# Output projection in two passes for the first and last chunk only, in whole tiles for the two in between; second passes and two last-projection tiles moved

## The chip, the cores and the metric

The kernel runs on all 8 NeuronCores of one Trainium2 chip. Each core takes one of the 8 sequences (2048 tokens of width 1024), so the cores do the same work on other data and do not talk to each other. The time is device microseconds of the slowest core, the median of several executions. TensorE (PE in the rows) multiplies, VectorE (DVE) and ScalarE (ACT) read its results out of the eight PSUM banks, GpSimd (POOL) works on SBUF alone, and SyncE (SP) issues the DMAs.

## The reference, cut to what matters

```python
def ffn(x):                      # rank-256 feed-forward, hidden width 4096
    P = x @ U1
    H = gelu(P @ V1 + b1)
    Q = H @ U2
    return Q @ V2 + b2
x = x + 0.5 * ffn(layernorm(x))
y = layernorm(x)                 # attention: 16 heads of 64, causal
q, k, v = y @ Q_w + Q_b, y @ K_w + K_b, y @ V_w + V_b
attn = softmax(mask(q @ k.T / 8)) @ v
x = x + attn @ O_w + O_b         # the output projection: 1024 x 1024
x = x + 0.5 * ffn(layernorm(x))
```

## The kernel before, in words

Everything is held transposed, features on partitions and tokens along the row. The 2048 tokens are four **chunks** of 512; a 1024-wide row is eight blocks of 128 features, so `x[:, c, m, :]` is chunk c, block m. A matmul has at most 512 columns, which fill one PSUM bank.

The kernel has three stages: a first feed-forward (chunk by chunk), attention (two heads at a time, eight **head pairs** p = 0 to 7), and a second feed-forward. Each engine has its own queue, filled by the Python program in a fixed order; an engine runs its queue strictly in that order, and a wait stops everything behind it on that engine.

**Attention** goes in 40 **rounds** to a head pair. Round k issues the scores of two key tiles (`qk_step`, line 1036), ScalarE's exponential of them (line 1049), and, three rounds late (`LAG`), the product with V (`av_step`, line 1074). Scores use banks 0 to 3, so the scores of round i wait for the exponential of round i-2. The products use banks 4 and 5. At the end of one head of one chunk ScalarE takes the logarithm and the exponential of the sums (lines 1090 and 1095) and VectorE multiplies them in (line 1099, `multiply`). In the last pair the chunks come in order: chunk 0 has rounds 0 to 3, chunk 1 rounds 4 to 11, chunk 2 rounds 12 to 23, chunk 3 rounds 24 to 39. ScalarE has more to do in a round than TensorE, so other TensorE work is pulled into the rounds from a generator (`window`, in the last pair `window7`), by shares that `spread` works out in units of one 512-column matmul. That work uses banks 6 and 7: `main_bank` takes them in turn, `side_bank` names the other one.

**The output projection** needs all eight pairs: 32 tiles (c, m) of eight matmuls, one for each pair. Before the change every tile has two passes: `o_most` does the seven pairs that are there early and VectorE adds bank and bias to x (line 1242); `o_last` does the matmul of the last pair when its chunk is ready (line 1250), and VectorE adds that too (line 1252). `o_last` starts for chunks 0, 1 and 2 at rounds 9, 17 and 29 (`O_GATE`), for chunks 1 and 2 also not before the normalisation of chunk 0 has come to its stage 3; between two `o_last` an `o_most` is issued as long as there are any. The last two of the 32 `o_most` are kept for the end, after round 39. The eight `o_last` of chunk 3 follow them: five at once, three in the first steps of the feed-forward.

In between, `window7` also prepares the second feed-forward for chunk 0: `ln3_cast` (VectorE's copy to bf16, line 179, and GpSimd's square, line 187) for every two blocks, two sums on TensorE (`ln_sum`, line 195), and the projection with U1 (line 227).

**The second feed-forward** takes 32 **steps** to a chunk. Step g has two V1 matmuls (lines 254 and 256) into bank g mod 3, ScalarE's gelu (line 261), and two U2 matmuls for step g-2 (line 271) into banks 3 and 4. `put(c, s, ...)` hangs further work on step s of chunk c, behind its V1 matmuls and ahead of its U2 matmuls. The last projection of chunk c-1 (`out_tile`: two V2 matmuls at lines 289 and 291, VectorE's sum at line 296, and the store of the result) hangs on steps 4 to 11 of chunk c. `f2_stat` at step 18 and `f2_break` at step 21 normalise the next chunk: ScalarE leaves its gelu table for logarithm and exponential, TensorE does 16 U1 matmuls, VectorE scales them out of banks 6 and 7 (line 237).

Of the kernel before, what the change touches and what calls it, by code (L numbers as in the profile page):

```python
# [17 lines left out]
NP = 8  # L18
# [67 lines left out]
def build_nc(debug=()):  # L86
# [1033 lines left out]
    def window(p):  # L1120
# [8 lines left out]
        if p == NP - 2:  # L1129
            mains += [(lambda: o_most(*o_left.popleft())) for _ in range(3)]  # L1130
        after = {}
# [95 lines left out]

    def o_most(c, m):

        b = main_bank()  # L1230
        PE.need(t_wo[m], bank_free[b])
        t = None
        for k in range(NP - 1):
            PE.need([t_at[k, c, h] for h in range(2)])
            f = lambda e, k=k: e.matmul(ps[:, b, :], wo[:, m, k, :], attn[:, c, k, :], start=(k == 0), stop=(k == NP - 2))  # L1235
            if k < NP - 2:
                PE.run(f)
                yield 1
            else:
                t = PE.do(f)  # L1240
        DVE.need(t, t_cols)
        bank_free[b] = DVE.do(lambda e: e.scalar_tensor_tensor(  # L1242
            x[:, c, m, :], ps[:, b, :], cols[:, C_OB + m:C_OB + m + 1], x[:, c, m, :], OP.add, OP.add))
        yield 1

    def o_last(c, m, b=None):

        b = main_bank() if b is None else b
        PE.need(t_wo[m], bank_free[b], [t_at[NP - 1, c, h] for h in range(2)])
# [23 lines left out]

    o_left = collections.deque((c, m) for c in range(NCH) for m in WO)

    O_GATE = (9, 17, 29)

    def window7():


        last = collections.deque((c, n) for c in range(NCH - 1) for n in range(NM))
        stage, since, k1 = 0, 0, {}
        while o_left or last or stage < 6:
            moved = False
            if last and rounds[0] >= O_GATE[last[0][0]] and (last[0][0] == 0 or stage >= 3):
                c, n = last.popleft()
                assert (c, WO[n]) not in o_left
                yield from o_last(c, WO[n])
                if n % 2 and c < 2:
                    ln3_cast(c, WO[n] // 2)  # L1290
                if (c, n) == (0, NM - 1):
                    stage, since = 1, 0
                moved = True
            if stage == 1 and since >= 3:
                b1 = main_bank()
# [18 lines left out]
            elif stage in (4, 5) and since >= 2:  # L1314
# [6 lines left out]
                stage, since, moved = stage + 1, 1, True  # L1321
            if o_left and (len(o_left) > 2 or rounds[0] >= 40):
                yield from o_most(*o_left.popleft())
                since += 1
                moved = True
            if not moved:
# [49 lines left out]
    for i in range(len(steps) + LAG + 3):  # L1376
        if i < len(steps):
            p, c, h, r, n, it = steps[i]
            k = i - 40 * p
            if k == 0:  # L1380
# [163 lines left out]
```

How the kernel before makes its waits and increments, by code:

```python
    def need(self, *tokens):  # L41
        for t in tokens:
            if t is None:
                continue
            if isinstance(t, list):
                self.need(*t)
                continue
            sem, val = t
            if self.passed.get(id(sem), 0) >= val:
                continue
            self.passed[id(sem)] = val
            self.items.append(lambda e, sem=sem, val=val: e.wait_ge(sem, val))
# [1 line left out]
    def do(self, fn):  # L54
        self.n += 1
        self.items.append(lambda e, fn=fn: fn(e).then_inc(self.sem, 1))
        return (self.sem, self.n)
# [21 lines left out]
    def load(self, q, out, src):  # L80
        self.n += 16
        q.items.append(lambda e, out=out, src=src: e.dma_start(out, src).then_inc(self.sem, 16))
        return (self.sem, self.n)
```

## Time and profile before

| | |
|---|---|
| times of 3 runs, us | 876.78, 876.81, 903.51; median 876.81 |
| the profiled execution | 876.68 us, its slowest core's span 875.1 us (core 7) |
| spans of the 8 cores | 871.3 to 875.1 us |
| busy in that span | PE 821.2 us (94%), DVE 466.4 us (53%), ACT 636.8 us (73%), POOL 167.0 us (19%) |
| first scores of the last head pair | 613.10 us from the start |
| first U2 matmuls of the second feed-forward | 722.23 us from the start |

The profiled execution's own time is 1.6 us above its span, and 0.1 us from the median. A matmul's busy time (379 ns for 512 columns) overlaps the next one's: back to back they start 216 ns apart. So a hole between two of them is best counted from start to start, less 216 ns for each matmul in between; the idle time that a row prints in brackets is 0.16 us shorter.

### The profile page before, as it was taken

The numbers are of one execution on the slowest core, as the hardware profiler recorded it, in microseconds if no ns is written. First come the engines' busy times: TensorE is split into PE (matmuls) and PEld (weight loads), VectorE is DVE, ScalarE is ACT, GpSimd is POOL, SyncE is SP. The second block draws the span as 40 slices with busy tenths as digits, with TensorE's granted clock in tenths as the row PEclk, the third lists the DMA queues.
The fourth block names the chain that finished last, engine by engine and source line by source line (L and its number), as shares of the span: only waits on it lengthen the run. The fifth ranks groups of instructions, "written<-read, shape, count | busy, mean of one in ns | idle before, by whom it ended". The sixth has DMA issues, their size and how long they took to land.

```text
span 875.1 us, 13105 instructions; the slowest of 8 cores (871.3 to 875.1 us)
## 1 busy us (share of the span) xinstructions
PE 821.2 (94%) x4122; PEld 397.4 (45%) x4122; DVE 466.4 (53%) x735; ACT 636.8 (73%) x803; POOL 167.0 (19%) x192
## 2 busy tenths in 40 slices
PE   4899999999899999999999999999989969999997
PEld 1344444444445455464554545544434424444442
DVE  2466665656565744746447474374553470445352
ACT  2667675768566898999999898989646526766764
POOL 0220400003231212313123131221231220031100
PEclk9899999999999999999999999999999999999999
DMA  8899301000041002200012000227000010122122
GB/s 266 265 324 322 54 2 49 1 2 1 1 119 40 1 1 55 78 25 1 1 61 73 25 1 1 75 73 239 26 1 1 1 41 8 46 64 88 22 97 96
DMA packets 17929, 57.83 MB, mean 66 GB/s; under 512 B 2116, under 2 KB 3524, under 8 KB 17352
## 3 DMA queue, kind: packets, MB, share of 16 engines
q1 hardware_dynamic: 17864, 57.00, 21.6%
q8 instruction: 36, 0.59, 0.3%
q14 instruction: 29, 0.24, 0.1%
HBM read 43.35 MB, written 13.64 MB: 65 GB/s over the span
## 4 chain that ended last, share of the span: by engine, by line
PE 85%; DVE 6%; ACT 4%; issue 3%; DMA 1%; DVEq 0%; SPq 0%; POOL 0%; ACTq 0%; POOLq 0%
PE ps L1036 13%; PE ps L271 13%; PE ps L1074 12%; PE ps L673 12%; PE ps L254 6%; PE ps L256 6%; PE ps L822 6%; PE ps L1235 6%; PE ps L195 4%; PE ps L227 2%; ACT pt L1049 2%; PE ps L730 1%; PE ps L289 1%; PE ps L291 1%; DMA x<-x 1%
## 5 line engine op out<-in xcount | busy, mean ns | idle before, releaser
L1049 ACT ACTIVATE pt<-ps,small 128x1024 bf16<-128x1024 f32 x320 | 321.8, 1026 | 97.6 <-PE ps L1036 91.3
L261 ACT ACTIVATE hb<-ps,cols 128x512 bf16<-128x512 f32 x256 | 171.3, 686 | 80.2 <-PE ps L256 79.3
L1036 PE MATMUL ps<-QZ,KM 128*128 128x512 bf16 (+1 forms) x640 | 177.1, 358 | 2.0 <-ACT pt L1049 1.8
L1074 PE MATMUL ps<-pt,V 128*128 128x512 bf16 (+3 forms) x640 | 170.3, 348 | 0.9 <-POOL V L884 0.9
L1058 POOL TENSOR_TENSOR pt<-pt,cb 128x256 bf16<-128x256 bf16 x128 | 87.3, 694 | 335.6 <-ACT pt L1049 335.6
L673 PE MATMUL ps<-yb,wqk 128*128 128x512 bf16 x512 | 140.3, 382 | 4.2 <-DVE small L734 1.5
L1074 PEld LDWEIGHTS ps<-pt,V 128*128 128x128 bf16 x640 | 62.5, 98 | 66.6 <-issue 2.1
L1036 PEld LDWEIGHTS ps<-QZ,KM 128*128 128x128 bf16 x640 | 61.1, 98 | 61.8 <-issue 13.7
L271 PE MATMUL ps<-hb,u2b 128*128 128x512 bf16 x256 | 76.5, 384 | 3.7 <-ACT hb L261 2.1
L271 PE MATMUL ps<-hb,u2c 128*128 128x512 bf16 x256 | 75.3, 379 | 1.8 <-ACT hb L261 1.4
L822 PE MATMUL ps<-wvb,yb 128*128 128x256 bf16 x512 | 73.5, 272 | 1.9 <-DVE small L734 1.2
L673 PEld LDWEIGHTS ps<-yb,wqk 128*128 128x128 bf16 x512 | 48.5, 98 | 53.0 <-issue 8.4
L296 DVE SCALAR_TENSOR_TENSOR x<-ps,small,x 128x512 f32<-128x512 f32 x64 | 47.2, 749 | 35.9 <-PE ps L291 35.8
L696 DVE TENSOR_SCALAR QZ<-ps,cols 64x512 bf16<-64x512 f32 x64 | 47.9, 748 | 33.5 <-PE ps L673 32.1
L734 DVE TENSOR_REDUCE small<-ps 128x1 f32<-128x512 f32 x64 | 44.1, 689 | 34.4 <-PE ps L730 33.9
L1235 PE MATMUL ps<-attn,wo 128*128 128x512 bf16 x224 | 57.1, 379 | 4.7 <-DVE x L1242 4.7
L822 PEld LDWEIGHTS ps<-wvb,yb 128*128 128x128 bf16 x512 | 49.0, 99 | 25.8 <-issue 3.9
L1099 DVE TENSOR_TENSOR attn<-ps,LR 64x512 bf16<-64x512 f32 x64 | 44.0, 688 | 30.9 <-ACT LR L1095 28.3
L254 PE MATMUL ps<-pb,v1b 128*128 128x512 bf16 x128 | 50.0, 390 | 3.3 <-DVE small L465 3.3
L256 PE MATMUL ps<-pb,v1b 128*128 128x512 bf16 x128 | 49.9, 390 | 0.0
L256 PE MATMUL ps<-pb,v1c 128*128 128x512 bf16 x128 | 48.5, 379 | 0.0
L254 PE MATMUL ps<-pb,v1c 128*128 128x512 bf16 x128 | 48.5, 379 | 0.0
(134 smaller groups left out, 876.5 us busy)
## 6 DMA issues: line engine op xcount, KB each, us to landing
x<-x SPq DMA_DIRECT2D x16, 512.0 KB, 13.2
out<-x SPq DMA_DIRECT2D x32, 256.0 KB, 2.4
stg<-u SPq DMA_DIRECT2D x10, 512.0 KB, 10.9
stg<-v SPq DMA_DIRECT2D x10, 512.0 KB, 10.8
wos<-wo SPq DMA_DIRECT2D x8, 512.0 KB, 4.2
wst<-wq SPq DMA_DIRECT2D x7, 512.0 KB, 4.0
wst<-wk SPq DMA_DIRECT2D x7, 512.0 KB, 4.3
wst<-wv SPq DMA_DIRECT2D x6, 512.0 KB, 10.2
```

What stands on the lines that cost most here:

```text
L254: PE.run(lambda e: e.matmul(ps[:, b, :], F["v1"][:, fc // 4, 0, 128 * (fc % 4):128 * (fc % 4 + 1)], F["pb"][:, c % 2, 0, :], start=True, s ...
L256: t = PE.do(lambda e: e.matmul(ps[:, b, :], F["v1"][:, fc // 4, 1, 128 * (fc % 4):128 * (fc % 4 + 1)], F["pb"][:, c % 2, 1, :], start=Fals ...
L261: F["t_gelu"][g] = ACT.do(lambda e: e.activation(F["hb"][:, g % 4, :], ps[:, b, :], AF.Gelu_apprx_tanh, bias=cols[:, C_B1 + fc:C_B1 + fc + ...
L271: f = lambda e, m=m: e.matmul(ps[:, 3 + m, :], F["u2"][:, fc, 128 * m:128 * (m + 1)], F["hb"][:, g % 4, :], start=(fc == 0), stop=(fc == N ...
L673: f = lambda e, k=k: e.matmul(ps[:, b, :], wqk[:, which, k, :], yb[:, ch, k, :], start=(k == 0), stop=(k == NM - 1))
L696: toks.append(DVE.do(lambda e, r=r, h=h: e.tensor_scalar(QZ[s][r, h, csl], ps[r, b, :], cols[r, C_QB + p:C_QB + p + 1], None, OP.add)))
L822: f = lambda e, k=k, kt=kt, o=o: e.matmul(ps[:, b, o:o + 256], yb[:, kt // 4, k, 128 * (kt % 4):128 * (kt % 4 + 1)], wvb[:, k, :], start=( ...
L1036: f = lambda e, j=j, kt=kt: e.matmul(ps[:, 2 * sl + j, lo:TC], KM[s][:, 128 * kt:128 * (kt + 1)], QZ[s][:, h, TC * c + lo:TC * (c + 1)], s ...
L1049: t_e[i] = ACT.do(lambda e: e.activation(pt[:, i % 4, :, lo:TC], ps[:, 2 * sl:2 * sl + 2, lo:TC], AF.Exp, bias=bias, scale=0.125))
L1058: L["pt", i] = POOL.do(lambda e, v=v: e.tensor_tensor(v, v, mask, OP.mult))
L1074: f = lambda e, kt=kt, lo=lo, j=j: e.matmul(ps[:, b, lo:TC], V[gr % 2][:, kt, pr, 64 * h:64 * h + 128], pt[:, i % 4, j, lo:TC], start=(kt ...
L1235: f = lambda e, k=k: e.matmul(ps[:, b, :], wo[:, m, k, :], attn[:, c, k, :], start=(k == 0), stop=(k == NP - 2))
```

## The change

- `o_most` becomes `o_tile(c, m, np)`, which does seven pairs or all eight. Chunks 1 and 2 are now done in whole tiles of eight matmuls with one addition on VectorE, from rounds 17 and 29 on. Chunks 0 and 3 keep their two passes (3 of the 16 first passes lie in pair 6 as before, 11 in the last pair ahead of the rest, and two are again kept for the end).
- The eight second passes of chunk 0 are no longer between tiles: they go inside a first pass, after its third and sixth matmul, into `side_bank`; when no first pass is left they go one after the other.
- The casts of chunk 1 for the normalisation are kept back until chunk 0 has reached stage 3. The waits in units between the stages of chunk 0 are two instead of three for the first.
- In the last three rounds two units are pulled instead of seven.
- The eight second passes of chunk 3 all hang on steps of the feed-forward's chunk 0: 3, 4, 5, 6, 22, 22, 23, 23.
- `out_tile` of blocks 6 and 7 moves from steps 10 and 11 to steps 22 and 23, both into bank 5, for the chunks 0 and 1 (which are put out during chunks 1 and 2).

```diff
@@ window
         if p == NP - 2:
-            mains += [(lambda: o_most(*o_left.popleft())) for _ in range(3)]
+            mains += [(lambda: o_tile(*o_most.popleft())) for _ in range(3)]
@@ the tile and the second pass
-    def o_most(c, m):
+    def o_tile(c, m, np=NP - 1):
         b = main_bank()
         PE.need(t_wo[m], bank_free[b])
         t = None
-        for k in range(NP - 1):
+        for k in range(np):
             PE.need([t_at[k, c, h] for h in range(2)])
-            f = lambda e, k=k: e.matmul(ps[:, b, :], wo[:, m, k, :], attn[:, c, k, :], start=(k == 0), stop=(k == NP - 2))
-            if k < NP - 2:
+            f = lambda e, k=k: e.matmul(ps[:, b, :], wo[:, m, k, :], attn[:, c, k, :], start=(k == 0), stop=(k == np - 1))
+            if k < np - 1:
                 PE.run(f)
                 yield 1
             else:
                 t = PE.do(f)
...
     def o_last(c, m, b=None):
-        b = main_bank() if b is None else b
+        b = side_bank() if b is None else b
@@ window7
-    o_left = collections.deque((c, m) for c in range(NCH) for m in WO)
+    o_most = collections.deque((c, m) for c in (0, NCH - 1) for m in WO)
+    O_END = 2
...
-        last = collections.deque((c, n) for c in range(NCH - 1) for n in range(NM))
+        full = collections.deque((c, m) for c in range(1, NCH - 1) for m in WO)
+        last = collections.deque(WO)
...
+        def last_one():
+            m = last.popleft()
+            yield from o_last(0, m)
+            if m % 2:
+                ln3_cast(0, m // 2)
+            if not last:
+                stage, since = 1, 0
...
-            if o_left and (len(o_left) > 2 or rounds[0] >= 40):
-                yield from o_most(*o_left.popleft())
+            while held and stage >= 3:
+                ln3_cast(1, held.popleft())
+            tile = None
+            if full and rounds[0] >= O_GATE[full[0][0]]:
+                c, m = full.popleft()
+                tile = o_tile(c, m, NP)
+            elif o_most and (len(o_most) > O_END or rounds[0] >= 40):
+                c, m = o_most.popleft()
+                tile = o_tile(c, m)
+            if tile is not None:
+                for u, _ in enumerate(tile):
+                    yield 1
+                    if u in (2, 5) and last and rounds[0] >= O_GATE[0] and (0, last[0]) not in o_most:
+                        yield from last_one()
+                if c == 1 and m % 2:
+                    held.append(m // 2)
                 since += 1
+                moved = True
+            elif last and rounds[0] >= O_GATE[0] and (0, last[0]) not in o_most:
+                main_bank()
+                yield from last_one()
                 moved = True
@@ the rounds after the last
-            pull(acc + 7)
+            pull(acc + 2)
@@ ahead of and in the second feed-forward
-    for n, b in enumerate((6, 7, 4, 3, 5)):
-        go(o_last(3, WO[n], b))
...
-    for n, b in ((5, 5), (6, 6), (7, 7)):
-        put(0, n - 4, lambda n=n, b=b: go(o_last(3, WO[n], b)))
+    for n, (g, b) in enumerate(((3, 5), (4, 6), (5, 7), (6, 5), (22, 5), (22, 6), (23, 7), (23, 5))):
+        put(0, g, lambda n=n, b=b: go(o_last(3, WO[n], b)))
     for c in range(NCH):
         if c >= 1:
             for m in range(8):
-                put(c, 4 + m, out_tile, c - 1, m, (7, 5, 6)[m % 3])
+                put(c, 4 + m if m < 6 else 16 + m if c + 1 < NCH else 4 + m, out_tile, c - 1, m,
+                    (7, 5, 6)[m % 3] if m < 6 or c + 1 == NCH else 5)
```

The line numbers of the changed kernel are a little higher: its tiles are at line 1236 with VectorE's sum at line 1243, its second passes at line 1254 with the sum at line 1256, its `mean_in` at line 1479.

**VectorE, rounds 9 to 12 of the last pair** (the second passes of chunk 0). `TENSOR_TENSOR x<-ps,x` is the sum of a second pass, `SCALAR_TENSOR_TENSOR x<-ps,cols,x` that of a first pass, `CAST xb3a<-x` the copy of two blocks for the normalisation, `attn<-ps,LR` is `multiply`. Before:

```order
L1242 SCALAR_TENSOR_TENSOR x<-ps,cols,x 128x512
L1252 TENSOR_TENSOR x<-ps,x 128x512
L179 CAST xb3a<-x 128x1024
L1242 SCALAR_TENSOR_TENSOR x<-ps,cols,x 128x512
L1252 TENSOR_TENSOR x<-ps,x 128x512
L1099 TENSOR_TENSOR attn<-ps,LR_81 64x512
```

Now:

```order
L1243 SCALAR_TENSOR_TENSOR x<-ps,cols,x 128x512
L1256 TENSOR_TENSOR x<-ps,x 128x512 x2
L179 CAST xb3a<-x 128x1024
L1243 SCALAR_TENSOR_TENSOR x<-ps,cols,x 128x512
L1256 TENSOR_TENSOR x<-ps,x 128x512 x2
L179 CAST xb3a<-x 128x1024
L1243 SCALAR_TENSOR_TENSOR x<-ps,cols,x 128x512
L1256 TENSOR_TENSOR x<-ps,x 128x512 x2
L1099 TENSOR_TENSOR attn<-ps,LR_81 64x512
```

A first pass's sum now stands behind a second pass's sum and a cast; before, it stood ahead of the second pass.

**TensorE, rounds 10 to 12**, where the second passes of chunk 0 lie. `L1036` are the scores of a round, `L1074` the product with V of three rounds earlier, `L1235` (now `L1236`) first-pass matmuls, `L1250` (now `L1254`) second passes. Before:

```order
L1235 MATMUL ps<-attn,wo 128x512 x2
L1250 MATMUL ps<-attn,wo 128x512
L1235 MATMUL ps<-attn,wo 128x512 x4
L1036 MATMUL ps<-QZ_71,KM_73 128x256 x2
L1074 MATMUL ps<-pt,V_70 128x512 x2
L1235 MATMUL ps<-attn,wo 128x512 x3
L1250 MATMUL ps<-attn,wo 128x512
L1235 MATMUL ps<-attn,wo 128x512 x3
```

Now:

```order
L1236 MATMUL ps<-attn,wo 128x512
L1254 MATMUL ps<-attn,wo 128x512
L1236 MATMUL ps<-attn,wo 128x512 x4
L1254 MATMUL ps<-attn,wo 128x512
L1036 MATMUL ps<-QZ_71,KM_73 128x256 x2
L1074 MATMUL ps<-pt,V_70 128x512 x2
L1236 MATMUL ps<-attn,wo 128x512 x3
L1254 MATMUL ps<-attn,wo 128x512
L1236 MATMUL ps<-attn,wo 128x512
L1254 MATMUL ps<-attn,wo 128x512 x2
```

Before, every second pass stood between two first passes. Now of the four first-pass matmuls in one piece the first ends a tile and the other three begin the next, in the other bank; the second pass behind them goes to the bank of the tile that has just ended. Two second passes of round 12 follow behind that round's scores and product, and no first pass is left.

**TensorE, rounds 13 to 17.** Before, rounds 13 to 16 had six to eight matmuls each beside the attention's. Now:

```order
L1074 MATMUL ps<-pt,V_70 128x256
L1074 MATMUL ps<-pt,V_70 128x128
L1036 MATMUL ps<-QZ_71,KM_73 128x512 x2
L1074 MATMUL ps<-pt,V_70 128x512 x2
L1036 MATMUL ps<-QZ_71,KM_73 128x512 x2
L1074 MATMUL ps<-pt,V_70 128x512 x2
L1036 MATMUL ps<-QZ_71,KM_73 128x256 x2
L1074 MATMUL ps<-pt,V_70 128x512 x2
L1236 MATMUL ps<-attn,wo 128x512 x16
L195 MATMUL ps<-xb3a,cb 128x512 x8
L1236 MATMUL ps<-attn,wo 128x512 x10
```

Rounds 13 to 16 have nothing beside the attention's matmuls, and round 17 has 34 others in one piece.

**TensorE, from the last round to the feed-forward's first U2 matmuls** (`L254` and `L256` are its V1 matmuls, `L271` its U2 matmuls). Before:

```order
L1235 MATMUL ps<-attn,wo 128x512 x7
L1074 MATMUL ps<-pt,V_70 128x512
L1074 MATMUL ps<-pt,V_70 128x384
L1235 MATMUL ps<-attn,wo 128x512 x7
L1074 MATMUL ps<-pt,V_70 128x256
L1074 MATMUL ps<-pt,V_70 128x128
L1250 MATMUL ps<-attn,wo 128x512 x5
L254 MATMUL ps<-pb_88,v1c 128x512
```

Now:

```order
L1236 MATMUL ps<-attn,wo 128x512 x2
L1074 MATMUL ps<-pt,V_70 128x512
L1074 MATMUL ps<-pt,V_70 128x384
L1236 MATMUL ps<-attn,wo 128x512 x2
L1074 MATMUL ps<-pt,V_70 128x256
L1074 MATMUL ps<-pt,V_70 128x128
L1236 MATMUL ps<-attn,wo 128x512 x10
L254 MATMUL ps<-pb_88,v1c 128x512
```

Ten matmuls of first passes now stand behind the last product, where five second passes stood; the first second pass of chunk 3 comes after the eight V1 matmuls of steps 0 to 3.

## Rows read from the trace of the kernel before

**Rows 1.** The page: chain that ended last, by engine.

```profile
PE 85%; DVE 6%; ACT 4%; issue 3%; DMA 1%; DVEq 0%; SPq 0%; POOL 0%; ACTq 0%; POOLq 0%
```

**Rows 2.** Timeline of TensorE: start us, duration us, engine, line, operation, count.

```profile
613.10 0.59 PE L1036 MATMUL ps<-QZ,KM 128*128 128x512 bf16 x2
...
619.64 1.89 PE L1235 MATMUL ps<-attn,wo 128*128 128x512 bf16 x8
```

**Rows 3.** Timeline of all engines, around one second pass of chunk 0.

```profile
651.53 0.69 DVE L179 CAST xb3a<-x 128x1024 bf16<-128x1024 f32 x1
...
652.92 0.59 PE L1235 MATMUL ps<-attn,wo 128*128 128x512 bf16 x2
653.35 0.38 PE L1250 MATMUL ps<-attn,wo 128*128 128x512 bf16 x1
653.62 0.75 DVE L1242 SCALAR_TENSOR_TENSOR x<-ps,cols,x 128x512 f32<-128x512 f32 x1 [0.67 <-PE ps L1235]
...
654.52 0.81 PE L1235 MATMUL ps<-attn,wo 128*128 128x512 bf16 x3 [0.79 <-DVE x L1242]
```

**Rows 4.** Waits between 610 and 720 us: who waited, for whom, total us, times, longest.

```profile
PE ps L1235 <- DVE x L1242: 4.7, 6, 0.8
...
PE ps L1250 <- DVE x L1252: 3.0, 6, 1.6
```

**Rows 5.** Timeline, second passes of chunks 1 and 2.

```profile
705.73 1.19 PE L1250 MATMUL ps<-attn,wo 128*128 128x512 bf16 x2 [1.61 <-DVE x L1252]
```

**Rows 6.** Windows: stretch, length, each engine's busy us (x), granted clock, DMA.

```profile
706.00:707.00 1.00, 0.99 (x4) 0.44 (x4) 0.76 (x2) 0.00 (x0) 1.00 (x1) 0.50 0.00 0
...
760.00:780.00 20.00, 20.00 (x94) 9.11 (x93) 10.04 (x13) 10.98 (x17) 7.84 (x4) 1.00 0.35 119
```

**Rows 7.** Timeline, from the last product of attention to the feed-forward.

```profile
714.28 0.33 PE L1074 MATMUL ps<-pt,V 128*128 128x256 bf16 x2
...
714.76 0.59 ACT L1090 ACTIVATE LR<-ps 64x512 f32<-64x512 f32 x1 [6.64 <-PE ps L1074]
...
717.01 1.24 PE L1250 MATMUL ps<-attn,wo 128*128 128x512 bf16 x5 [2.40 <-DVE attn L1099]
...
717.38 0.20 ACT L1425 ACTIVATE small<-small 128x1 f32<-128x1 f32 x1
...
720.72 0.38 PE L1250 MATMUL ps<-attn,wo 128*128 128x512 bf16 x1 [1.61 <-DVE x L1252]
...
722.23 1.03 PE L271 MATMUL ps<-hb,u2c 128*128 128x512 bf16 x4
```

**Rows 8.** The page's group of the exponential; timeline of one round's scores and exponential.

```profile
L1049 ACT ACTIVATE pt<-ps,small 128x1024 bf16<-128x1024 f32 x320 | 321.8, 1026 | 97.6 <-PE ps L1036 91.3
...
641.28 0.59 PE L1036 MATMUL ps<-QZ,KM 128*128 128x512 bf16 x2
...
641.97 1.11 ACT L1049 ACTIVATE pt<-ps,small 128x1024 bf16<-128x1024 f32 x1 [2.12 <-PE ps L1036]
```

**Rows 9.** Timeline, end of the feed-forward's chunk 0 (steps 22 to 24).

```profile
745.46 1.29 DVE L237 TENSOR_TENSOR pb<-ps,rstd 128x512 bf16<-128x512 f32 x2 [5.43 <-ACT rstd L219]
745.54 0.38 PE L254 MATMUL ps<-pb,v1c 128*128 128x512 bf16 x1
...
746.22 1.28 ACT L261 ACT_TABLE_LOAD   x1 [0.86 <-PE ps L256]
...
747.51 2.64 ACT L261 ACTIVATE hb<-ps,cols 128x512 bf16<-128x512 f32 x4
...
748.34 0.59 PE L271 MATMUL ps<-hb,u2c 128*128 128x512 bf16 x2 [0.48 <-ACT hb L261]
```

**Rows 10.** Timeline, VectorE's sum of one second pass, the next one, and a V2 tile's sum.

```profile
700.92 0.68 DVE L1252 TENSOR_TENSOR x<-ps,x 128x512 f32<-128x512 f32 x1
...
701.75 0.38 PE L1250 MATMUL ps<-attn,wo 128*128 128x512 bf16 x1 [0.22 <-DVE x L1252]
...
759.71 0.75 DVE L296 SCALAR_TENSOR_TENSOR x<-ps,small,x 128x512 f32<-128x512 f32 x1 [2.21 <-PE ps L291]
```

More of the change, by code:

```diff
@@ L1241, in o_most @@
         DVE.need(t, t_cols)
-        bank_free[b] = DVE.do(lambda e: e.scalar_tensor_tensor(
+        t = DVE.do(lambda e: e.scalar_tensor_tensor(
             x[:, c, m, :], ps[:, b, :], cols[:, C_OB + m:C_OB + m + 1], x[:, c, m, :], OP.add, OP.add))
+        bank_free[b] = t
+        if np == NP:
+            t_x2[c][m] = t
         yield 1
     def o_last(c, m, b=None):
-        b = main_bank() if b is None else b
+        b = side_bank() if b is None else b
         PE.need(t_wo[m], bank_free[b], [t_at[NP - 1, c, h] for h in range(2)])
@@ L1272, in ffn2_weights @@
         F2["t_u1"] = ld_sc[2].load(SP, u1c[:, :, :], s_u1)
-    o_left = collections.deque((c, m) for c in range(NCH) for m in WO)
+    o_most = collections.deque((c, m) for c in (0, NCH - 1) for m in WO)
     O_GATE = (9, 17, 29)
+    O_END = 2
     def window7():
-        last = collections.deque((c, n) for c in range(NCH - 1) for n in range(NM))
-        stage, since, k1 = 0, 0, {}
-        while o_left or last or stage < 6:
-            moved = False
[L1285 to L1294, printed above, removed]
+        full = collections.deque((c, m) for c in range(1, NCH - 1) for m in WO)
+        last = collections.deque(WO)
+        stage, since, k1, held = 0, 0, {}, collections.deque()
+        def last_one():
+            nonlocal stage, since
+            m = last.popleft()
+            assert (0, m) not in o_most
+            yield from o_last(0, m)
[3 more added lines that the diff above has]
+                stage, since = 1, 0
+        while o_most or full or last or held or stage < 6:
+            moved = False
+            if stage == 1 and since >= 2:
                 b1 = main_bank()
@@ L1397, in build_nc @@
                 else:
-                    share = spread(p, 0, 40, 7 * len(o_left) - 14 + 24 + 32)
+                    share = spread(p, 0, 40, 7 * (len(o_most) - O_END) + 8 * 16 + 8 + 32)
             rounds[0] = k if p == NP - 1 else 0
```

## The prediction

> **What bounds the kernel now.** The chain of waits comes first: 85% of the span goes through TensorE [rows 1], and the feed-forwards run it without a hole, 20.00 us of 20.00 at full clock in a stretch of the second [rows 6]. The change touches the last head pair and what follows, so I read TensorE's timeline there. From the pair's first scores at 613.10 [rows 2] to the feed-forward's first U2 matmuls at 722.23 [rows 7] are 109.1 us. A 512-column matmul costs 0.216 us: eight in a row took 1.89, the last one's 0.38 included [rows 2]. The program has the work of 419.5 such matmuls in that stretch (203 first-pass and 32 second-pass matmuls, 16 for sums, 16 U1, 8 V1, and 144.5 for the attention), 90.6 us. So 18.5 us are holes, and the reader should see in the rows that they are of three kinds.
>
> - **A: a tile after a second pass.** VectorE's sum of a first pass starts 0.49 us after the last matmul (652.92 plus 0.22, to 653.62) and the next tile, two banks on and so in the same bank, starts 0.90 us after that; one second pass of 0.22 stands between. The hole is 654.52 - 653.35 - 0.22 = 0.95 [rows 3]. The list of waits has six of this kind for first passes, 4.7 us in brackets [rows 4]; five lie beside chunk 0's second passes, and with one for the U1 matmuls and smaller ones A is 7.4 us.
> - **B: sixteen second passes with hardly a first pass between them**, 700 to 711 us. One matmul of 0.22 needs a sum of 0.68 [rows 10], and two banks don't hide that; the longest single hole is 1.77 us, 1.61 in brackets, where casts stood among the sums [rows 5]. Behind it the granted clock was 0.50, which is 1.2 GHz, and matmuls took twice their time [rows 6]. B is 6.5 us.
> - **C: the end.** The last product ends at 714.28 + 0.16 = 714.44 (call it T). Five second passes wait for the last `multiply` until 717.01, and a sixth for sums until 720.72 [rows 7]. From T to 722.23 are 7.8 us for 16 matmuls, 3.5 us: 4.3 us of holes.
>
> ScalarE waits for TensorE 91.3 us at its exponentials over the whole kernel [rows 8], so in general a hole that closes on TensorE is time won.
>
> **The change part by part.**
>
> *Whole tiles for chunks 1 and 2.* The sixteen second passes, and their sixteen sums, go; the matmuls stay, as eighth of a tile. A bank comes back after 8 matmuls in the other one, 1.7 us, against the 0.49 + 0.90 of A. B goes, and so do the holes of A that don't belong to chunk 0 (one first pass, the U1 matmuls). I leave 0.6 us for small ones (such as a sum held up by a cast of 0.69 [rows 3]). GpSimd's squares and masks are off this path, as the product comes three rounds late.
>
> *The second passes of chunk 0 inside tiles.* They don't get cheaper. Take the order on VectorE: second-pass sum, cast (every second time), first-pass sum. From t = 0, the second of them in round 10: its sum runs 0.48 to 1.16, and 0.15 later the next tile may use its bank (701.60 to 701.75 in [rows 10]), at 1.31; one matmul stood between, so 0.88 us of hole. The cast goes to 1.82, the ended tile's sum to 2.55, so the second pass behind three matmuls starts at 2.70 instead of 1.96: 0.74. Scores, product and three matmuls hide the next. The fourth pass is at 4.21; its sum, its cast and the last first pass's sum end at 6.78, and the fifth starts at 6.93 instead of 4.65: 2.28. The last one waits 0.43 more. Sum 4.3 us, where before the same eight cost 5.1.
>
> *Rounds 13 to 16 without other work.* From the start of round 13's scores to that of round 17's, TensorE has four rounds of scores and four products, two of them short ones at the diagonal: 3.1 us. ScalarE starts an exponential 0.69 us after the scores begin [rows 8], and does three of 1.03 and a logarithm of 0.59 [rows 7] before round 17's scores may start: 0.69 + 3.09 + 0.6 = 4.4. So TensorE loses 1.25 us. It can't be below 0, and is 3 if the other closing steps of chunk 1 and their latencies fall into it too. I take 1.25. The 34 matmuls of round 17 cost nothing: ScalarE waits, and has the time for it afterwards.
>
> *The end.* Behind T now stand ten first-pass matmuls and V1 of steps 0 to 3. ScalarE is through with its table and a small gelu at 717.38 + 0.20, that is T + 3.14 [rows 7]. V1 of step 0 is done by T + 2.6 plus latency, so gelu 0 runs to T + 3.83. V1 of step 3 uses its bank and starts at T + 3.97; ahead of it are 16 matmuls, 3.46: a hole of 0.5. Then 0.43, a second pass of 0.22, and U2 starts at T + 4.6. Of C 4.3 becomes 0.5.
>
> Here the Trainium skill differs from the trace. In the trace a table load is 1.28 us and the next activation follows at once [rows 9]; "ScalarE: Activation LUTs", section "What ACT_TABLE_LOAD costs", has about 2.66 us, because a drain of 1.38 comes on top. By that, an estimate from the page, the hole would be 1.9 instead of 0.5 and the time 1.4 us longer; by this trace there is no such gap.
>
> *The feed-forward.* Seven second passes that were in the stretch are now inside steps: the stretch loses 1.5 us of work and the feed-forward gets it, sum 0. In steps 3 to 6 they have a bank each and VectorE is idle. At the end of a chunk the U2 matmuls of step 22 wait for gelu 22 behind a table load; the hole is 0.48, or 0.64 from start to start [rows 9]. Work of 0.86 us put there is partly free. Chunk 0's four second passes need banks 6 and 7, which VectorE scales until 746.75 [rows 9]; TensorE comes to them at 746.2 and 747.3, so they hardly wait, and U2 starts at 748.63 instead of 748.34: 0.57 won. For chunks 1 and 2 both V2 tiles use bank 5: the first one's sum of 0.75 [rows 10] stands behind the scaling, 746.75 to 747.5, so the second starts at 747.62 instead of 747.26, and U2 at 748.9: 0.3 won each. Together 1.2; between 0 (if the sums come later than this) and 1.9.
>
> **Sum.** The stretch: 412.5 matmuls are 89.1 us, and 4.3 + 1.25 + 0.5 + 0.6 = 6.65 of holes, 95.8 against 109.1: 13.4 less, of which 1.5 has only moved: 11.9. With 1.2, 13.1 us. The profiled execution took 876.7, as the median (876.8), so 863.7.
>
> **The rivals.**
>
> *The holes are larger than worked out, 868 us.* Rounds 10 to 16 have 5.6 us of holes close together. Before, the clock went to 1.2 GHz behind such a stretch (B) and cost 1.7 us; for it speaks that likeness, against it that the holes of A and of C left the clock at full. The Trainium skill, "TensorE: Matmul & The Clock Gate", section "A second HAM failure mode: psum-queue depth-cycling", says that small idle times between groups that cycle through banks can make the clock go up and down; of its two cases here, A and B, the trace has it in B. With the clock 1.7, rounds 13 to 16 at 3 instead of 1.25, and nothing from the feed-forward, 1.2: 868.4. Chance 0.2.
>
> *The second passes of chunk 0 are hidden after all, 859.5.* If VectorE's queue were not in the way, 4.3 us of holes would go. For it: they were put into the other bank, three matmuls and a round's attention apart. Against: the order of casts and sums. Chance 0.09.
>
> *The change doesn't do what it says, 874.* Whole tiles could meet holes as before: if each waits for VectorE 0.6 us, 16 tiles take back 10 of the 13 us. Against: 1.7 us of cover, and 16 sums fewer. Chance 0.04.
>
> *Slower, above 877.* The one mechanism is rounds 12 to 16: TensorE falls to ScalarE's pace, the clock goes to 1.2 GHz and stays there. A matmul then costs twice; from a saving of 13.1 us, it decides when more than 26 us run at 1.2 GHz. In this trace the low clock held about 3.4 us in B, and it rose while matmuls ran densely; the 34 in one piece behind the gap are dense. Chance 0.01.
>
> **How the numbers follow.** The forecast has 0.66. It spans 860.5 to 866.5 by its own bounds: the feed-forward's gain, rounds 13 to 16, and 1.5 us either way on the holes of rounds 10 to 12. The range takes in the larger holes above and most of the hidden case: 859.5 to 869.5. A measurement can tell about 2% from no change, 17.5 us here: faster than 859.3 takes a part of the hidden case and little else, 0.05; slower than 894 needs the last rival, and far more than 26 us of it, under 0.01; the rest, 0.94, is within 2%.
>
> **What the changed profile would show.** No line for second passes between rounds 17 and 39, and no clock of 0.5 near 700; waits of tiles for VectorE's sums only in rounds 10 to 12, one of them 2 us long or more; in rounds 13 to 16 scores waiting for exponentials, about a microsecond in all; U2 4.6 us behind the last product; at the end of chunks 1 and 2 of the feed-forward a V2 matmul that waits a third of a microsecond for a sum. The stretch from the pair's first scores to U2 should be 95.8 us. Wrong would be the step on rounds 10 to 16 above all: it is worked out from an order, and the order of VectorE's and ScalarE's turns moves with every hole.

## The result, and the profile after

| | before | changed |
|---|---|---|
| profiled execution, us | 876.68 | 866.92 |
| span of its slowest core, us | 875.1 | 865.4 |
| spans of the 8 cores, us | 871.3 to 875.1 | 856.2 to 865.4 |
| median, us | 876.8 (3 runs; a fourth, run beside the changed kernel, took 957.03) | 866.2 (4 runs: 865.15, 865.44, 866.92, 956.6) |

The ratio is 0.9869, with a 95% interval of 0.9842 to 0.9895: 1.3% or 11.5 us faster, clear of the noise though less than 2%. It leaves out the runs in a disturbed state of the chip (903.51, 957.03 and 956.6), which both kernels have. The forecast was 863.7 us, ratio 0.985, with 859.5 to 869.5.

Most of the work below goes by two lengths on one core. The **long stretch** is from attention's first scores to the second feed-forward's first U2 matmuls; it holds the last head pair. The **feed-forward** is from there to its last U2 matmuls. Both are read from the starts of the rows, and both repeat from core to core within 0.1 us where the granted clock doesn't fall to 1.2 GHz on the way (the falls come below). Here is the profile of the changed kernel, timeline of TensorE on core 3, which had no such fall:

```profile
203.77 0.59 PE L1036 MATMUL ps<-QZ,KM 128*128 128x512 bf16 x2
...
709.88 0.59 PE L271 MATMUL ps<-hb,u2c 128*128 128x512 bf16 x2
```

709.88 - 203.77 = 506.1 us. Before, on core 5, likewise without a fall (timeline of TensorE):

```profile
202.68 0.59 PE L1036 MATMUL ps<-QZ,KM 128*128 128x512 bf16 x2
...
720.77 0.59 PE L271 MATMUL ps<-hb,u2c 128*128 128x512 bf16 x2
```

518.1 us. So 12.0 us came from the long stretch. The feed-forward got longer by 0.44, from 141.22 to 141.66 us. That is 11.6 us, about the 11.5 of the ratio.

**Where the 12.0 us are.** At the end of attention, timeline of all engines on core 1, the answer to [rows 7]:

```profile
707.44 0.33 PE L1074 MATMUL ps<-pt,V 128*128 128x256 bf16 x2
707.60 2.32 PE L1236 MATMUL ps<-attn,wo 128*128 128x512 bf16 x10
...
709.25 1.28 ACT L1455 ACT_TABLE_LOAD   x1
...
710.54 0.20 ACT L1455 ACTIVATE small<-small 128x1 f32<-128x1 f32 x1
...
710.65 2.41 ACT L261 ACTIVATE hb<-ps,cols 128x512 bf16<-128x512 f32 x4
...
711.47 0.38 PE L254 MATMUL ps<-pb,v1c 128*128 128x512 bf16 x1 [0.25 <-ACT hb L261]
...
712.11 1.03 PE L271 MATMUL ps<-hb,u2c 128*128 128x512 bf16 x4
```

From the last product's end at 707.60 to U2 are 4.5 us instead of 7.8, with one hole of 0.41 (711.47 less 710.84, the start of the last V1 matmul, less 0.22). The ten matmuls cover ScalarE's way to the gelu. The table load ends at 710.53; the small activation and the gelus follow it directly, as in [rows 9].

Between 654 and 707 us TensorE has hardly a hole left. The windows of core 1 answer to [rows 6]:

```profile
646.00:648.00 2.00, 2.00 (x7) 0.61 (x6) 2.00 (x4) 1.12 (x1) 0.49 (x1) 0.55 0.00 0
...
660.00:680.00 20.00, 20.00 (x99) 9.32 (x97) 7.89 (x11) 12.30 (x14) 7.18 (x5) 1.00 0.00 1
690.00:704.00 14.00, 14.00 (x68) 6.43 (x66) 4.49 (x7) 8.60 (x9) 0.14 (x1) 1.00 0.01 2
```

So B is gone, and so are the holes of A from chunk 1 on. But in the first row the clock is 0.55 (1.2 GHz for most of it), at another place than before. On four cores before and two after, it also fell near 224 us, at the start of attention, which made their long stretches 1.6 to 1.8 us longer. The slowest core of each profile had both falls.

What is left stands in rounds 10 to 16, here on core 3 (timeline of TensorE and VectorE; the pattern of before is [rows 3]):

```profile
636.66 0.38 PE L1254 MATMUL ps<-attn,wo 128*128 128x512 bf16 x1
636.87 0.38 PE L1236 MATMUL ps<-attn,wo 128*128 128x512 bf16 x1
637.14 0.69 DVE L1256 TENSOR_TENSOR x<-ps,x 128x512 f32<-128x512 f32 x1 [0.77 <-PE ps L1254]
...
637.94 1.07 DVE L179 CAST xb3a<-x 128x1024 bf16<-128x1024 f32 x1
637.98 0.81 PE L1236 MATMUL ps<-attn,wo 128*128 128x512 bf16 x3 [0.73 <-DVE x L1256]
638.93 0.74 DVE L1243 SCALAR_TENSOR_TENSOR x<-ps,cols,x 128x512 f32<-128x512 f32 x1
639.82 0.38 PE L1254 MATMUL ps<-attn,wo 128*128 128x512 bf16 x1 [1.03 <-DVE x L1243]
...
641.54 0.38 PE L1236 MATMUL ps<-attn,wo 128*128 128x512 bf16 x1
...
642.61 0.69 DVE L179 CAST xb3a<-x 128x1024 bf16<-128x1024 f32 x1
643.22 0.75 DVE L1243 SCALAR_TENSOR_TENSOR x<-ps,cols,x 128x512 f32<-128x512 f32 x1
644.11 0.59 PE L1254 MATMUL ps<-attn,wo 128*128 128x512 bf16 x2 [2.19 <-DVE x L1243]
...
646.03 0.38 PE L1254 MATMUL ps<-attn,wo 128*128 128x512 bf16 x1 [0.22 <-DVE x L1256]
...
648.19 0.59 PE L1036 MATMUL ps<-QZ,KM 128*128 128x512 bf16 x2 [0.38 <-ACT pt L1049]
...
650.95 0.38 PE L1036 MATMUL ps<-QZ,KM 128*128 128x256 bf16 x2 [0.73 <-ACT pt L1049]
```

The reader should see the order on VectorE: second pass's sum, cast, first pass's sum, and that TensorE's next second pass starts only behind the third. From start to start the holes are 0.89, 1.19, 2.35 and 0.38 us, 4.8 together; then scores wait for exponentials, 0.55, 0.15 and 0.89, 1.6 together.

**In the feed-forward**, the end of chunk 1 (core 1, timeline; [rows 9] before):

```profile
775.09 1.28 ACT L261 ACT_TABLE_LOAD   x1 [0.85 <-PE ps L256]
...
775.62 0.75 DVE L296 SCALAR_TENSOR_TENSOR x<-ps,small,x 128x512 f32<-128x512 f32 x1
775.92 0.38 PE L256 MATMUL ps<-pb,v1c 128*128 128x512 bf16 x1
...
776.51 0.38 PE L289 MATMUL ps<-qm,v2c 128*128 128x512 bf16 x1 [0.21 <-DVE x L296]
```

The wait of U2 for the gelu is filled. The second V2 tile waits 0.37 us for the first one's sum in the same bank.

### The profile page after: what moved, and what is told of

It is laid out like the page before. It is cut to its first block, busy times and chain, and to the rows that moved or that the text cites. A ratio compares the mean times of both kernels' runs of the same rounds, so it can differ in the third digit from the quotient of the medians.

```text
span 865.4 us, 13056 instructions; the slowest of 8 cores (856.2 to 865.4 us)
## 1 busy us (share of the span) xinstructions
PE 821.1 (95%) x4122; PEld 398.3 (46%) x4122; DVE 460.8 (53%) x719; ACT 638.3 (74%) x803; POOL 167.0 (19%) x192
## 4 chain that ended last, share of the span: by engine, by line
PE 83%; DVE 5%; ACT 5%; issue 4%; DMA 1%; DVEq 0%; SPq 0%; POOL 0%; ACTq 0%; POOLq 0%
PE ps L1036 13%; PE ps L271 12%; PE ps L673 12%; PE ps L1074 12%; PE ps L254 6%; PE ps L256 6%; PE ps L1236 5%; PE ps L822 5%; PE ps L195 4%; ACT pt L1049 2%; PE ps L289 1%; PE ps L730 1%; PE ps L291 1%; PE ps L227 1%; PE ps L427 1%
## 5 line engine op out<-in xcount | busy, mean ns | idle before, releaser
L1036 PE MATMUL ps<-QZ,KM 128*128 128x512 bf16 (+1 forms) x640 | 177.4, 359 | 3.0 <-ACT pt L1049 2.8
L1074 PE MATMUL ps<-pt,V 128*128 128x512 bf16 (+3 forms) x640 | 170.6, 348 | 0.9 <-POOL V L884 0.9
L1074 PEld LDWEIGHTS ps<-pt,V 128*128 128x128 bf16 x640 | 62.5, 98 | 67.3 <-issue 3.2
L1036 PEld LDWEIGHTS ps<-QZ,KM 128*128 128x128 bf16 x640 | 61.0, 98 | 63.7 <-issue 16.2
L271 PE MATMUL ps<-hb,u2b 128*128 128x512 bf16 x256 | 77.4, 388 | 3.9 <-ACT hb L261 2.1
L271 PE MATMUL ps<-hb,u2c 128*128 128x512 bf16 x256 | 75.3, 379 | 0.3
L1236 PE MATMUL ps<-attn,wo 128*128 128x512 bf16 x240 | 60.1, 379 | 0.7 <-DVE x L1256 0.7
L254 PE MATMUL ps<-pb,v1b 128*128 128x512 bf16 x128 | 50.3, 393 | 3.3 <-DVE pb L237 3.3
L256 PE MATMUL ps<-pb,v1b 128*128 128x512 bf16 x128 | 50.3, 393 | 0.0
L254 PE MATMUL ps<-pb,v1c 128*128 128x512 bf16 x128 | 48.5, 379 | 0.2 <-ACT hb L261 0.2
L256 PE MATMUL ps<-pb,v1c 128*128 128x512 bf16 x128 | 48.5, 379 | 0.0
```

The lines of the kernel that those rows point to most:

```text
L254: PE.run(lambda e: e.matmul(ps[:, b, :], F["v1"][:, fc // 4, 0, 128 * (fc % 4):128 * (fc % 4 + 1)], F["pb"][:, c % 2, 0, :], start=True, s ...
L256: t = PE.do(lambda e: e.matmul(ps[:, b, :], F["v1"][:, fc // 4, 1, 128 * (fc % 4):128 * (fc % 4 + 1)], F["pb"][:, c % 2, 1, :], start=Fals ...
L271: f = lambda e, m=m: e.matmul(ps[:, 3 + m, :], F["u2"][:, fc, 128 * m:128 * (m + 1)], F["hb"][:, g % 4, :], start=(fc == 0), stop=(fc == N ...
L1036: f = lambda e, j=j, kt=kt: e.matmul(ps[:, 2 * sl + j, lo:TC], KM[s][:, 128 * kt:128 * (kt + 1)], QZ[s][:, h, TC * c + lo:TC * (c + 1)], s ...
L1074: f = lambda e, kt=kt, lo=lo, j=j: e.matmul(ps[:, b, lo:TC], V[gr % 2][:, kt, pr, 64 * h:64 * h + 128], pt[:, i % 4, j, lo:TC], start=(kt ...
```

## The experiments

The table has the cores on which the clock fell nowhere in the long stretch (the last row has none, see there); "feed-forward" is the same on all eight cores within 0.02 us.

| kernel | long stretch, us | feed-forward, us | product to U2, us | ratio to before |
|---|---|---|---|---|
| before | 518.1 | 141.22 | 7.8 | |
| end alone | 512.7 | 142.20 | 4.5 | 0.9946 (0.9928 to 0.9965) |
| changed | 506.1 | 141.66 | 4.5 | 0.9869 (0.9842 to 0.9895) |
| changed, run again | 506.0 | 141.66 | 4.5 | 0.9868 (0.9854 to 0.9882) |
| cast behind the tile's sum | 504.05 | 141.65 | 4.5 | one run, 861.75 us |
| even shares | 503.5 | 141.66 | 4.5 | 0.9831 (0.9815 to 0.9846) |
| inner chunks whole | 497.8 | 143.38 | 4.45 | 0.9778 (0.9754 to 0.9801) |
| the same, two details more | 497.8 | 142.42 | 4.45 | 0.9771 (0.9755 to 0.9788) |
| casts twice | 508.6, with a fall | 141.65 | 4.5 | one run, 866.95 us |

### The end alone

```diff
--- before
-            pull(acc + 7)
+            pull(acc + 2)
-    for n, b in enumerate((6, 7, 4, 3, 5)):
-        go(o_last(3, WO[n], b))
-    for n, b in ((5, 5), (6, 6), (7, 7)):
-        put(0, n - 4, lambda n=n, b=b: go(o_last(3, WO[n], b)))
+    for n, (g, b) in enumerate(((3, 5), (4, 6), (5, 7), (6, 5), (22, 5), (22, 6), (23, 7), (23, 5))):
+        put(0, g, lambda n=n, b=b: go(o_last(3, WO[n], b)))
```

> The kernel before with one part of the change: all eight second passes of chunk 3 in steps 3, 4, 5, 6, 22, 22, 23, 23 of the second feed-forward, and two units instead of seven pulled in the last rounds. Theory (the end is a term of its own, 4.3 us of holes down to 0.5): from the last product to U2 4.5 us instead of 7.8; the stretch from the last pair's first scores to U2 103.8 us (109.1, less 3.8 of holes and 1.5 of moved matmuls) with the holes between tiles and the chain of second passes near 700 us as before; the second feed-forward 142.2 us; in all about 4.4 us faster than before. Rival (the end's holes only become holes elsewhere, as ScalarE's table and gelus pace it anyway): U2 not earlier than 7 us behind the last product, total within 1 us of before.

Measured: 4.5 us from product to U2, the long stretch 5.4 us shorter (expected 3.8 + 1.5), the feed-forward 142.20. In all 518.1 + 141.2 to 512.7 + 142.2, 4.4 us, as expected; the rival falls. The list of waits from 610 to 716 us shows the holes of A and B untouched, with the numbers of [rows 4]:

```profile
PE ps L1235 <- DVE x L1242: 4.7, 6, 0.8
...
PE ps L1250 <- DVE x L1252: 3.0, 6, 1.6
```

This run also splits the feed-forward. It has seven second passes more than before, 1.51 us of matmuls, and is 0.98 longer: 0.53 were free at the end of chunk 0. The changed kernel differs from it there only in the V2 tiles, and has 0.54 less: 0.27 a chunk.

### The cast behind the tile's own sum

```diff
--- changed
 def last_one():
             yield from o_last(0, m)
             if m % 2:
-                ln3_cast(0, m // 2)
+                casts.append(m // 2)
...
+                while casts:
+                    ln3_cast(0, casts.popleft())
```

(the last two lines behind the whole first pass, and behind a second pass that stands alone)

> The changed kernel, with the cast that follows every other second pass of chunk 0 put behind the sum of the tile it lies in. Theory (VectorE's order makes the long holes of rounds 10 to 12: a first pass's bank waits behind a cast of 0.69 us): the holes of 1.2 and 2.3 us become about 0.5 and 1.6, the stretch 94.5 us on a core whose clock does not fall, against 95.9. Rival (the two banks alone make them, in whatever order VectorE works): holes and stretch as in the changed kernel, 95.9.

Measured: 504.05 against 506.1, 2.0 us less on core 0 and on every core without a fall; with the last pair starting at 609.5 the stretch is 94.0. Timeline of core 0:

```profile
632.39 0.38 PE L1236 MATMUL ps<-attn,wo 128*128 128x512 bf16 x1
...
633.50 0.81 PE L1236 MATMUL ps<-attn,wo 128*128 128x512 bf16 x3 [0.73 <-DVE x L1256]
...
634.15 0.38 PE L1254 MATMUL ps<-attn,wo 128*128 128x512 bf16 x1
...
635.94 0.38 PE L1236 MATMUL ps<-attn,wo 128*128 128x512 bf16 x1
...
637.71 0.59 PE L1254 MATMUL ps<-attn,wo 128*128 128x512 bf16 x2 [1.39 <-DVE x L1243]
```

The second hole is gone (634.15 follows 633.50 by three matmuls), the third is 1.55 instead of 2.35, the first and the fourth are what they were. The cast's place on VectorE is the cause of the second hole and of 0.8 us of the third, more than expected because one cast had taken 1.07 us and not 0.69. The other 2.8 us stay: the cast isn't their cause. The clock fell on none of the eight cores in the last pair.

### Casts twice

```diff
--- changed
             if m % 2:
+                DVE.need(t_x2[0][m - 1:m + 1], L.get(("xb3f", 0)))
+                tx = DVE.do(lambda e, i=m // 2: e.tensor_copy(xb3[0][:, 2 * i:2 * i + 2, :], x[:, 0, 2 * i:2 * i + 2, :]))
+                DVE.need(tx)
                 ln3_cast(0, m // 2)
```

> The changed kernel with each cast of chunk 0 done twice in a row, to the same place: the suspected cost doubled. Theory (a first pass's bank waits behind the cast, and the holes bring the clock down): the two holes behind casts grow by 0.7 us each, to 1.9 and 3.1 us, the clock falls on all 8 cores, stretch 97.4 us without its cost and 98.5 with it; the first hole (0.9 us, behind no cast) stays. Rival (the holes are the banks' alone): stretch as in the changed kernel, 95.9 to 97.0.

Measured on core 0 (timeline):

```profile
633.37 0.38 PE L1236 MATMUL ps<-attn,wo 128*128 128x512 bf16 x1
...
634.47 0.81 PE L1236 MATMUL ps<-attn,wo 128*128 128x512 bf16 x3 [0.73 <-DVE x L1256]
...
637.11 0.38 PE L1254 MATMUL ps<-attn,wo 128*128 128x512 bf16 x1 [1.83 <-DVE x L1243]
...
642.26 1.01 PE L1254 MATMUL ps<-attn,wo 128*128 128x512 bf16 x2 [2.98 <-DVE x L1243]
```

and in the windows of that core

```profile
640.00:642.00 2.00, 0.00 (x0) 0.00 (x0) 1.90 (x3) 0.00 (x0) 0.40 (x1) 0.93 0.00 0
642.00:644.00 2.00, 1.74 (x5) 0.66 (x6) 1.16 (x3) 0.00 (x0) 1.49 (x1) 0.50 0.00 0
```

The holes behind casts are 2.0 and 3.15 us (0.8 more each, the second copy and its wait), the first still 0.89. The clock fell on all eight cores, on two of them for twice as long (6.8 us, long stretch 509.9) and on one twice (510.4). Five cores have 508.6 to 508.9, where the last pair takes 98.5 to 98.8, as expected. Both experiments on the cast say the same from either side.

### Even shares

```diff
--- changed
-                    share = spread(p, 0, 40, 7 * (len(o_most) - O_END) + 8 * 16 + 8 + 32)
+                    early = 7 * (len(o_most) - O_END) + 8
+                    share = spread(p, 0, 40, early + 8 * 16 + 32)
+                    at16, end = share[16], share[39]
+                    for j in range(40):
+                        share[j] = (share[j] * early / at16 if j <= 16 else
+                                    early + (share[j] - at16) * (end - early) / (end - at16))
```

> The changed kernel, with the shares of the last pair's rounds scaled so that the first passes and second passes of chunk 0 last until round 16 (about five matmuls a round instead of seven and then none). Theory (rounds 13 to 16 cost 1.2 us because nothing is left to pull, and the crowding of second passes in rounds 10 to 12 costs most of the 4.9 us there): no scores wait for an exponential in these rounds, the second passes stand apart with attention between them, holes from round 9 to 17 together 2 to 3 us instead of 6.5, the clock does not fall there, stretch 91.5 to 93 us on every core. Rival (second passes cost their holes wherever they stand between tiles): holes of 4 us and more remain, stretch 94.5 us.

Measured: 503.5, 2.6 us less than the changed kernel, a stretch of 93.4. No scores wait for an exponential between rounds 9 and 17, and no clock falls in the last pair. But five holes stay at the second passes, 0.89, 0.93, 0.89, 0.46 and 0.52, 3.7 us: more than the 2 to 3 expected, less than the 4 of the rival. The stretch lies between the 93 of the theory and the 94.5 of the rival. The three long ones have one picture (core 1, timeline):

```profile
636.10 0.38 PE L1236 MATMUL ps<-attn,wo 128*128 128x512 bf16 x1
...
636.37 0.69 DVE L1256 TENSOR_TENSOR x<-ps,x 128x512 f32<-128x512 f32 x1 [0.18 <-PE ps L1254]
...
637.21 0.59 PE L1236 MATMUL ps<-attn,wo 128*128 128x512 bf16 x2 [0.73 <-DVE x L1256]
```

A second pass behind the sixth matmul of a tile leaves one matmul until the next tile wants its bank. Filling the rounds is worth the 1.6 us of waits for exponentials and 1.1 of the 4.8, less a new hole of 0.27 near 617 us. The three long holes, 2.7 us, go with the place of the second pass in the tile; no run moved it within the tile.

### Inner chunks whole

Two passes for chunks 2 and 3, whole tiles for 0 and 1, so that no second pass lies between tiles.

```diff
--- changed
-    o_most = collections.deque((c, m) for c in (0, NCH - 1) for m in WO)
+    o_most = collections.deque((c, m) for c in (2, 3) for m in WO)
-        full = collections.deque((c, m) for c in range(1, NCH - 1) for m in WO)
-        last = collections.deque(WO)
+        full = collections.deque((c, m) for c in range(2) for m in WO)
-                    share = spread(p, 0, 40, 7 * (len(o_most) - O_END) + 8 * 16 + 8 + 32)
+                    share = spread(p, 0, 40, 7 * (len(o_most) - O_END) + 8 * 16 + 32)
-    for n, (g, b) in enumerate(((3, 5), (4, 6), (5, 7), (6, 5), (22, 5), (22, 6), (23, 7), (23, 5))):
-        put(0, g, lambda n=n, b=b: go(o_last(3, WO[n], b)))
+    for n in range(8):
+        put(0, 3 + n, lambda n=n: go(o_last(2, WO[n], 5 + n % 3)))
+    for n, (g, b) in enumerate(((11, 7), (12, 5), (13, 6), (14, 7), (22, 5), (22, 6), (23, 7), (23, 5))):
+        put(0, g, lambda n=n, b=b: go(o_last(3, WO[n], b)))
```

(and the casts of chunk 0 behind its whole tiles; `last_one` goes)

> Two passes for chunks 2 and 3, whole tiles for chunks 0 and 1 (from rounds 9 and 17), all sixteen second passes in the second feed-forward's steps: chunk 2's in steps 3 to 10, chunk 3's in 11 to 14, 22, 22, 23, 23. Theory (second passes cost nothing beside their matmul in a feed-forward step, and up to 0.95 us of hole each between tiles): stretch 88.5 us on every core (404.5 matmuls are 87.4) with no fall of the clock, second feed-forward 143.4 us (8 matmuls more than in the changed kernel), in all 5.7 us less than the changed kernel on cores without a fall of the clock and 7.5 on those with one, so about 858.5 us. Rival (VectorE or the banks in the feed-forward's steps can't take them): the second feed-forward grows by more than 4 us and the gain is under 3 us.

Measured: 857.4 us, ratio 0.9778 (0.9754 to 0.9801). The last pair takes 87.7 us, the feed-forward 143.38, 1.72 more than in the changed kernel where eight matmuls are 1.73: second passes there cost their matmul and nothing else. The rival falls. No clock fell in the last pair.

### The same with two details more, and the changed kernel again

```diff
--- inner chunks whole
-        put(0, 3 + n, lambda n=n: go(o_last(2, WO[n], 5 + n % 3)))
+        put(0, 2 + n, lambda n=n: go(o_last(2, WO[n], 5 + n % 3)))
-                    (7, 5, 6)[m % 3] if m < 6 or c + 1 == NCH else 5)
+                    (7, 5, 6)[m % 3] if m < 6 or c + 1 == NCH else m - 1)
```

> The kernel with whole tiles for chunks 0 and 1 and all second passes in the feed-forward, and two details more: chunk 2's second passes one step earlier (steps 2 to 9), and the V2 tile of block 7 into bank 6 instead of bank 5. Theory: the hole at the V1 matmul of step 3 (0.34 us) closes; the second V2 tile at the ends of chunks 1 and 2 no longer waits for the first one's sum, 0.36 us each; stretch 87.7 us (work that moves ahead of U2 adds what the hole gives), second feed-forward 142.3 to 142.7 us, 0.7 to 1.1 us less in all than with the details left out; ratio to before 0.976 to 0.978. Rival (gelu 22 behind its table load ends the wait anyway): the feed-forward stays at 143.4 us.

Measured: 855.3 us, ratio 0.9771 (0.9755 to 0.9788); the feed-forward 142.42, 0.96 less, of which 0.22 is the second pass that now lies ahead of U2 and 0.74 the two V2 tiles. Core 1, timeline at the end of chunk 1:

```profile
762.28 0.38 PE L256 MATMUL ps<-pb,v1c 128*128 128x512 bf16 x1
762.50 0.38 PE L289 MATMUL ps<-qm,v2c 128*128 128x512 bf16 x1
```

The V2 matmul follows at 0.22. The gain over the kernel without the details is below what the intervals can tell; the traces show it.

> The changed kernel once more, beside the others. Theory (the change is worth 11 to 12 us, and its clock still falls for 3.4 us in rounds 10 to 13 on most cores, which costs 1.1): ratio to before 0.986 to 0.988; stretch 95.9 us on cores without that fall and 97.0 on those with it, at least four of eight with it. Rival (the fall was an accident of the first profile): two cores or fewer have it.

Measured: ratio 0.9868 (0.9854 to 0.9882), 506.0 us on two cores and 507.0 to 507.3 on six. These six have the fall of the clock in rounds 10 to 13; the rival falls. On the same chip, the best version took 855.3 us and the changed kernel 864.2.

## What held in the prediction, and the step that failed

The time lies in the range, and the holes were found where they were forecast, each of the large ones within half a microsecond of its size. The step that failed is the sum's comparison of two stretches at different clocks; it comes after the parts that held.

- **The end (C).** Forecast 4.6 us from product to U2 with a hole of 0.5; measured 4.5 with 0.41. The experiment on it alone gave its 4.4 us. In this trace too the next activation follows a table load at once. The Trainium skill ("ScalarE: Activation LUTs", section "What ACT_TABLE_LOAD costs") has 2.66 us with a drain, which by estimate would have left a hole of 1.9 us; the trace doesn't bear it out.
- **Whole tiles (B and part of A).** No tile waits for VectorE from round 13 on, as forecast. Between the end alone and the changed kernel the long stretch is 6.6 us shorter on like cores: 7.8 us of holes behind round 13 go, and rounds 9 to 16 have 6.4 us of holes instead of 5.0.
- **Rounds 10 to 12.** Forecast holes of 0.88, 0.74, 2.28 and 0.43; measured 0.89, 1.19, 2.35 and 0.38, 4.8 instead of 4.3. The casts put behind and the casts doubled show the part that VectorE's order has in the second and the third. The 0.45 on the second hole comes with a cast that took 1.07 us instead of 0.69.
- **Rounds 13 to 16.** Forecast 1.25, measured 1.6.
- **Small holes.** Forecast 0.6; on core 3 there were less than 0.1.
- **The feed-forward.** Forecast 0.57 and 0.3 twice, so 0.3 us longer; measured 0.53 and 0.27 twice, 0.44 longer.

**The step that failed is the comparison in the sum, "95.8 against 109.1: 13.4 less".** It takes the changed stretch at full clock and the stretch of before from a core whose clock had fallen to 1.2 GHz in B [rows 6]. So it books the end of that fall as a gain, and puts a fall in the changed kernel's rounds 10 to 13 at nothing. Like with like the runs show 12.2 us: 108.1 to 95.9 on cores without a fall there, 109.1 to 97.0 with one. Windows before, core 5 and core 7 over the same 10 us (the first without, the second with the fall):

```profile
702.00:712.00 10.00, 7.00 (x30) 2.60 (x29) 8.29 (x12) 1.80 (x2) 5.49 (x4) 1.00 0.00 1
...
702.00:712.00 10.00, 7.26 (x25) 2.39 (x24) 7.95 (x12) 1.80 (x2) 5.49 (x4) 0.83 0.00 1
```

The fall costs 1.1 us by the long stretches (519.2 on a core with only this fall, 518.1 without), where the rival on larger holes had called it 1.7. Its end was no gain, as the fall only moved. Before, five of eight cores had it between 702 and 709 us. After, six of eight had it between 640 and 650 (507.2 against 506.1), and again six of eight when the kernel ran again. That rival named this mechanism, but not its time. The argument against it, that the holes of A left the clock at full, did not carry over: those are 0.95 us each and 3.3 us or more apart, while rounds 10 to 13 have 4.8 us of holes in about 9, like B with about 5.5 in 9.

With 1.1 for the clock, 0.5 and 0.35 for the holes of rounds 10 to 16, and 0.15 for the feed-forward, less 0.6 for the small holes that didn't come and 0.1 for the end, the forecast gives 865.1; measured by the ratio, 865.3. That the holes of the last pair came out right in all, 6.8 us against 6.65, is partly luck, as 0.85 too little and 0.7 too much nearly cancel.

**Why that cast took 1.07 us.** The rows point to GpSimd, though no run was made for it. Changed kernel, core 1, timeline of GpSimd, then of VectorE's casts:

```profile
638.95 0.67 POOL L1058 TENSOR_TENSOR pt<-pt,cb 128x256 bf16<-128x256 bf16 x1 [6.39 <-ACT pt L1049]
...
648.37 1.89 POOL L187 TENSOR_TENSOR sq<-xb3a 128x1024 bf16<-128x1024 bf16 x1 [1.88 <-DVE xb3a L179]
```

```profile
639.09 1.07 DVE L179 CAST xb3a<-x 128x1024 bf16<-128x1024 f32 x1
...
647.55 0.68 DVE L179 CAST xb3a<-x 128x1024 bf16<-128x1024 f32 x1
649.52 1.29 DVE L179 CAST xb3a<-x 128x1024 bf16<-128x1024 f32 x1
```

The first cast starts while GpSimd multiplies the causal mask in (until 639.62) and ends 0.54 us after it; the last starts during GpSimd's square (until 650.26) and ends 0.55 after it. Those with nothing beside them take 0.68 or 0.69. With the casts behind, core 0, they take 0.83, 0.87 and 1.29 us beside a mask and two squares, and each ends 0.55 after GpSimd. So a cast that meets a running GpSimd operation makes its way mostly when that has ended. The other way round, with even shares, a mask that starts 0.23 us into a cast takes 0.99 instead of 0.67. The trace of before had such a cast too, at B's longest hole (timeline of core 7):

```profile
702.54 1.89 POOL L187 TENSOR_TENSOR sq<-xb3b 128x1024 bf16<-128x1024 bf16 x1 [6.91 <-DVE xb3b L179]
...
703.70 1.29 DVE L179 CAST xb3b<-x 128x1024 bf16<-128x1024 f32 x1
```

The sum that [rows 5] waits for stands behind this cast. The prediction took every cast at 0.69 us, and these rows could have warned it. The Trainium skill ("SBUF — State Buffer", section "Who interferes with whom") says that a cast may take the port pair that VectorE shares with GpSimd, and that who comes first keeps the other out. The rows agree in both directions: 0.55 of a cast's 0.68 us come after GpSimd's end, and a GpSimd operation that comes second is longer too. That the shared ports are the reason wasn't tried by moving the mask, and stays open.

## What to carry to other kernels

A short piece of work that needs a PSUM bank should go where the engine that empties the bank is idle and the bank isn't asked for soon; here sixteen second passes cost no more than their own time in the feed-forward's steps, and eight cost up to 2.4 us of hole each between the tiles of a two-bank rotation. A cover that is worked out for TensorE has to be checked against the queue of the emptying engine, entry by entry: a cast of 0.7 us in between was 0.8 us of the longest hole. And where a sum compares a trace with a forecast, both must have the same clock, so the stretch of before is to be read on a core where it did not fall, and a fall in the new stretch is a term of its own.

## What the runs showed of the hardware

- The clock of a stretch with holes differed between cores of one run. In rounds 10 to 13, with 4.8 us of holes, it fell to 1.2 GHz on 6 of 8 cores (twice, in two runs of the changed kernel). With 2.8 us (casts behind) it fell on none, and with at least 6.0 us (casts twice) on all 8, on three of them for 6.8 us in all instead of 3.4.
- A fall of 3.4 us cost 1.1 us in such a stretch, where part of it lay over holes, and 1.6 to 1.8 us near 224 us, where the matmuls stood closer.
- VectorE's cast of 128x1024 took 0.68 or 0.69 us alone. Begun at least 0.13 us before the end of a GpSimd operation of 0.67 or 1.89 us, it took 0.74 to 1.29 and ended 0.55 us after it, in all 136 such casts between 600 and 710 us (all eight cores of seven profiles). A square of GpSimd that began 0.29 us into a cast took 2.15 us instead of 1.89, on all eight cores of the changed kernel.
- All else repeats closely: the feed-forward of the changed kernel took 141.65 or 141.66 us on each of the eight cores.
